# Mamba-2 mixer of a fused decoder layer: residual moved to ACT and GpSimd, and the order of the pass rewritten on five queues

## What is computed

```python
h = rmsnorm(x) * norm_w
z, xBC, dt = split(h @ in_proj_w.T)            # 1024, 1024+128+128, 16
xBC = silu(causal_conv4(xBC) + conv_b)         # depthwise, 4 taps
xs, B, C = split(xBC)
dt = softplus(dt + dt_bias); dA = exp(-exp(A_log) * dt)
state = state * dA_t + dt_t * outer(x_t, B_t)  # 16 heads of 64, state 128
y = state @ C_t + D * xs
y = rmsnorm(y * silu(z)) * ssm_norm_w
h1 = x + y @ out_proj_w.T
```

## Time and profile before

| what | us |
|---|---|
| median of 3 runs | 2724.34 (2722.08 to 2725.27) |
| the profiled execution, its own time | 2722.0 |
| span of the profiled execution | 2720.2 |
| PE busy | 2659.7 (98%) |
| DVE busy | 1523.4 (56%) |
| ACT busy | 1019.5 (37%) |
| POOL busy | 693.8 (26%) |

### The profile page before, as it was taken

One profiled execution on the slowest core, in us unless ns is written; L12 is line 12 of the kernel. 1 busy time (PEld: TensorE's weight loads), 2 busy tenths in 40 slices (PEclk: granted clock), 3 DMA queues, 4 the chain that ended last, 5 costly groups with the idle time before them and its releaser, 6 DMA issues.

```text
span 2720.2 us, 42348 instructions
## 1 busy us (share of the span) xinstructions
PE 2659.7 (98%) x15264; PEld 2070.4 (76%) x15264; DVE 1523.4 (56%) x2561; ACT 1019.5 (37%) x2375; POOL 693.8 (26%) x594
## 2 busy tenths in 40 slices
PE   7999999999999999999999989999999999999999
PEld 5777777777778888888888867777777777777776
DVE  8787797797795322332233277777777774111122
ACT  6334334334434222122212255555555553222221
POOL 6553553553561101000100101322233322000000
PEclk9999999999999999999999999999999999999999
DMA  4001001101114101110111211110111124211111
GB/s 154 27 21 47 31 15 46 44 3 46 46 48 140 62 1 62 62 62 0 62 62 48 73 70 48 63 40 29 62 54 62 58 64 150 82 47 46 46 46 47
DMA packets 85482, 147.83 MB, mean 54 GB/s; under 512 B 4032, under 2 KB 17984, under 8 KB 85408
## 3 DMA queue, kind: packets, MB, share of 16 engines
q1 hardware_dynamic: 85408, 146.84, 15.7%
HBM read 113.27 MB, written 33.55 MB: 54 GB/s over the span
## 4 chain that ended last, share of the span: by engine, by line
PE 88%; DVE 8%; issue 2%; ACT 1%; DMA 1%; DVEq 0%; SPq 0%; POOL 0%; ACTq 0%; POOLq 0%
PE ps L75 22%; PE ps L77 22%; PE ps L76 22%; PE ps L1770 4%; PE ps L2133 4%; PE ps L816 2%; PE ps L1782 2%; PE ps L1761 2%; DVE mx_m L608 1%; DVE mx_cv L600 1%; PE ps L792 1%; PE ps L804 1%; PE ps L747 1%; PE ps L1714 1%; PE ps L844 1%
## 5 line engine op out<-in xcount | busy, mean ns | idle before, releaser
L1471 ACT ACTIVATE at_pr<-ps,at_nm 128x256 f32<-128x256 f32 x512 | 235.6, 473 | 201.7 <-DVE at_nm L1621 201.7
L1162 DVE TENSOR_TENSOR gm_m_lo<-gm_m,gm_m_hi 128x512 fp32r<-128x512 f32 (+1 forms) x88 | 61.1, 694 | 416.9 <-ACT gm_m_hi L1079 416.9
L75 PE MATMUL ps<-sh_u_hi,gm_gu_hi 128*128 128x512 f32 (+1 forms) x704 | 274.9, 390 | 0.0
L76 PE MATMUL ps<-sh_u_lo,gm_gu_hi 128*128 128x512 f32 (+1 forms) x704 | 274.8, 390 | 0.0
L77 PE MATMUL ps<-sh_u_hi,gm_gu_lo 128*128 128x512 f32 (+1 forms) x704 | 274.7, 390 | 0.0
L1627 DVE COPY at_pT<-ps 128x512 f32<-128x512 f32 x256 | 176.3, 689 | 138.5 <-PE ps L1770 136.4
L1073 ACT ACTIVATE gm_sg<-ps 128x512 f32<-128x512 f32 (+1 forms) x88 | 52.7, 599 | 517.6 <-PE ps L77 517.4
L543 POOL TENSOR_TENSOR mx_m<-mx_m,mx_g 128x512 f32<-128x512 f32 x128 | 185.4, 1448 | 86.3 <-DVE mx_m L610 86.1
L75 PE MATMUL ps<-sh_u_hi,qm_w_hi 128*128 128x512 f32 x512 | 201.6, 394 | 2.1 <-issue 1.1
L77 PE MATMUL ps<-sh_u_hi,qm_w_lo 128*128 128x512 f32 x512 | 199.6, 390 | 0.0
L76 PE MATMUL ps<-sh_u_lo,qm_w_hi 128*128 128x512 f32 x512 | 199.4, 389 | 0.0
(11 more groups left out here) (252 smaller groups left out, 6352.6 us busy)
## 6 DMA issues: line engine op xcount, KB each, us to landing
sh_xf<-x_scratch SPq DMA_DIRECT2D x16, 1024.0 KB, 7.5
mx_xr<-in_x SPq DMA_DIRECT2D x8, 1024.0 KB, 5.6
h_scratch<-mx_xr SPq DMA_DIRECT2D x8, 1024.0 KB, 5.1
sh_xf<-h_scratch SPq DMA_DIRECT2D x8, 1024.0 KB, 8.4
gm_xr<-in_x SPq DMA_DIRECT2D x8, 1024.0 KB, 7.3
gm_r<-h_scratch SPq DMA_DIRECT2D x8, 1024.0 KB, 6.1
x_scratch<-gm_r SPq DMA_DIRECT2D x8, 1024.0 KB, 5.2
at_cf<-in_ctxT SPq DMA_DIRECT2D x16, 512.0 KB, 3.9
```

The costliest lines, as they stand in the source:

```text
L75: nc.tensor.matmul(out, l_hi, r_hi, start=first, stop=False)
L76: nc.tensor.matmul(out, l_hi, r_lo, start=False, stop=False)
L1471: A(pr[h][:, t, :], SC[h][:, SEQ * t:SEQ * t + SEQ], ACT.Exp, bias=nm[:, 4 * n + h, t:t + 1], accum_out=sums[:, 2 * b + t, 4 * g + h:4 * g ...
```

## The change

Residual: ACT scales the output product from PSUM into SBUF buffers `m0` (`scale_out`, two tiles behind the last work of a pass and two inside the next), POOL adds them to the input rows, in the order of tiles 2, 3, 0, 1; PE's projections n = 2 to 5 each wait for their own bank. Pass 7 keeps the old form. The squares of the next pass's input go from the convolutions into the head loop (j = 0 to 3), POOL's `first` goes behind head 9, and the normalisation goes from one tile at j = 1 to 4 to two tiles each at j = 5 and j = 6. DVE's `g_low(j - 1)` goes ahead of `scan(2j + 2)`, and PE's `chunk_out(j - 1)` ahead of `spread(2j + 4)`. The product of B and C goes ahead of projection 6, the first two spreads ahead of projection 8, the first two scans ahead of convolution 8. Convolution 9 goes on DVE behind the first gating, its SiLU on ACT behind the second.

```diff
@@ -343,9 +343,12 @@
...
-             "dac tap cv sl Ge z xd sc M t g gs glo acc sse rg h1").split()
+             "dac tap cv sl Ge z xd sc M t g gs glo acc sse rg ho h1").split()
...
+    OUT = (2, 3, 0, 1)
 
     def ahead(i):
 
@@ -462,6 +465,14 @@
             act.wait_ge(s["u"], i + 1)
             A(d["ln"], d["u"], ACT.Ln).then_inc(s["ln"], 1)
 
+        def scale_out(i, n):
+
+            t = OUT[n]
+            act.wait_ge(s["out"], KI * i + KI)
+            act.wait_ge(s["y"], KI * i + KI)
+            act.wait_ge(s["rg"], i + 1)
+            A(m0[t][:, :], ps[t][:, :], ACT.Copy, scale=rg[:, t:t + 1]).then_inc(s["ho"], 1)
+
         def main(i):
             if step_0(i):
                 take_dt(i)
@@ -469,12 +480,15 @@
             tap(i, 0)
             if step_0(i):
                 exp_ln(i)
+            else:
+                scale_out(i - 1, 2)
+                scale_out(i - 1, 3)
             tap(i, 1)
             act.wait_ge(s["dta"], i + 1)
             A(d["da"], d["dta"], ACT.Exp).then_inc(s["da"], 1)
             silu(i, 0)
             for n in range(2, NCONV - 1):
-                if n == NCONV - 2:
+                if n == NCONV - 3:
 
                     act.wait_ge(s["G"], i + 1)
                     at(act, s["M"], 2 * NH * i)
@@ -484,12 +498,9 @@
                 silu(i, n - 1)
                 if step_0(i):
                     wt.high(act, min(3 * KD + 2 * (n - 1), IN_PIECES))
-                if n >= 5:
-                    square(i + 1, n - 5)
+            zsilu(i, 0)
             silu(i, NCONV - 2)
-            zsilu(i, 0)
             tap(i, NCONV - 1)
-            silu(i, NCONV - 1)
             for j in range(KI):
                 if j + 1 < KI:
                     zsilu(i, j + 1)
@@ -504,14 +515,21 @@
                 else:
                     at(act, s["acc"], 7 * i + j - 1)
                 A(acc[:, :] if j == 0 else sq[:, :], zs[j % 2][:, :], ACT.Square).then_inc(s["gs"], 1)
-                if 1 <= j <= TT:
-                    norm(i + 1, j - 1)
+                if j == 1:
+                    silu(i, NCONV - 1)
+                if j < TT:
+                    square(i + 1, j)
+                elif j in (5, 6):
+                    norm(i + 1, 2 * j - 10)
+                    norm(i + 1, 2 * j - 9)
                 if final(i) and j >= 1:
 
                     me.nxt.wt.high(act, j if j <= 4 else 4 + 2 * max(j - 5, 0))
             if not final(i):
                 take_dt(i + 1)
                 exp_ln(i + 1)
+                scale_out(i, 0)
+                scale_out(i, 1)
 
         first(0)
         steps(act, main)
@@ -536,7 +554,6 @@
 
                 pool.wait_ge(su.small, smalls)
                 wt.by_pool(pool, len(pieces))
-            first(i + 1)
             pool.wait_ge(s["Ge"], 2 * i + 2)
             for h in range(NH):
                 pool.wait_ge(s["sc"], NH * i + h + 1)
@@ -544,10 +561,17 @@
                 G(m1[h % 4][:, :], m1[h % 4][:, :], g1[:, :], ALU.mult).then_inc(s["M"], 1)
                 if h % 2 == 1 and h >= 5:
                     add_squares(i, (h - 3) // 2)
+                if h == 9:
+                    first(i + 1)
             add_squares(i, 7)
-            at(pool, s["h1"], TT * i)
+            at(pool, s["ho"], TT * i)
             pool.wait_ge(s["sse"], i + 1)
             G(rg[:, :], v0[:, :], mhalf[:, :], ALU.pow).then_inc(s["rg"], 1)
+            if not final(i):
+                pool.wait_ge(s["xr"], 16 * i + 16)
+            for n, t in () if final(i) else enumerate(OUT):
+                pool.wait_ge(s["ho"], TT * i + n + 1)
+                G(xr[:, t, :], xr[:, t, :], m0[t][:, :], ALU.add).then_inc(s["h1"], 1)
 
         pool.wait_ge(su.dve, dve_0 + 4)
         first(0)
@@ -603,6 +627,9 @@
         def scan(i, h):
 
             dve.wait_ge(s["bc"], NH * i + h + 1)
+            if h == 0:
+
+                at(dve, s["h1"], TT * i)
             at(dve, s["y"], KI * i + h // 2 - 1)
             bank = BC[h % 2]
             V.tensor_tensor_scan(m0[h % 4][:, :], bank[:, :], eye0[:, :], 0.0, ALU.mult, ALU.add)
@@ -681,20 +708,20 @@
             for b in range(2):
                 V.memset(daT[0:2 * NH, SEQ * b:SEQ * b + 1].bitcast(F32), 0.0).then_inc(s["dac"], 1)
             for n in range(6, NCONV - 1):
+                if n == NCONV - 2:
+                    scan(i, 0)
+                    scan(i, 1)
                 conv(i, n)
                 if step_0(i):
                     wt.low(dve, 3 * KD + n - 1)
-            scan(i, 0)
-            scan(i, 1)
             scale_x(i, 0)
-            conv(i, NCONV - 1)
             if step_0(i):
                 wt.low(dve, IN_PIECES)
             for j in range(KI):
+                if j >= 1:
+                    g_low(i, j - 1)
                 if j + 1 < KI:
                     scan(i, 2 * j + 2)
-                if j >= 1:
-                    g_low(i, j - 1)
                 if j == KI - 1:
                     split(i + 1, 0)
                     split(i + 1, 1)
@@ -708,6 +735,8 @@
                 dve.wait_ge(s["z"], KI * i + j + 1)
                 dve.wait_ge(s["t"], KI * i + j + 1)
                 V.tensor_tensor(zs[j % 2][:, :], xc[:, j, :], zs[j % 2][:, :], ALU.mult).then_inc(s["g"], 1)
+                if j == 0:
+                    conv(i, NCONV - 1)
                 if final(i) and 2 <= j <= 5:
                     me.nxt.wt.low(dve, j - 1)
             split(i + 1, 2)
@@ -721,10 +750,12 @@
             V.tensor_scalar(v0[:, :], Y[:, 0:TT], 1.0 / DI, RMS_EPS, ALU.mult, ALU.add).then_inc(s["sse"], 1)
             if not final(i):
                 dt_second(i + 1)
-            dve.wait_ge(s["out"], KI * i + KI)
-            dve.wait_ge(s["xr"], 16 * i + 16)
-            dve.wait_ge(s["rg"], i + 1)
-            for t in range(TT):
+            if final(i):
+
+                dve.wait_ge(s["out"], KI * i + KI)
+                dve.wait_ge(s["xr"], 16 * i + 16)
+                dve.wait_ge(s["rg"], i + 1)
+            for t in range(TT) if final(i) else ():
                 V.scalar_tensor_tensor(xr[:, t, :], ps[t][:, :], rg[:, t:t + 1], xr[:, t, :], ALU.mult,
                                        ALU.add).then_inc(s["h1"], 1)
 
@@ -764,10 +795,10 @@
         def conv_in(i, n, also=None):
             if step_0(i) and n % 4 == 2:
                 pe.wait_ge(*wt.lows(n // 4 * KD + 2 * KD - 1))
+            if 2 <= n <= 5:
+                at(pe, s["ho"], TT * (i - 1) + n - 1)
             if n >= 4:
                 pe.wait_ge(s["cv"], 3 * NCONV * i + 3 * (n - 3))
-            elif n == 2:
-                at(pe, s["h1"], TT * i)
             project(CB[n], E_X + P * CH[n], also).then_inc(s["in"], 1)
 
         def z_in(i, c):
@@ -866,8 +897,6 @@
             for t in range(TT):
                 last = T.transpose(Y[0:2 * NH, P * t:P * t + P], da_hl[:, t, :].bitcast(F32), ident[:, :])
             last.then_inc(s["dat"], 1)
-            for n in range(6, NCONV - 2):
-                conv_in(i, n)
 
             at(pe, s["sc"], NH * i)
             pe.wait_ge(s["sl"], NCONV * i + 2)
@@ -876,10 +905,12 @@
                 T.matmul(BC[0][:, o:o + SEQ], bT[:, o:o + P], cT[:, o:o + SEQ], start=True, stop=True)
                 last = T.matmul(BC[1][:, P * b:P * b + P], bT[:, o + P:o + SEQ], cT[:, o + P:o + SEQ], start=True, stop=True)
             last.then_inc(s["G"], 1)
+            for n in range(6, NCONV - 2):
+                conv_in(i, n)
+            spread(i, 0)
+            spread(i, 1)
             conv_in(i, NCONV - 2)
             z_in(i, 0)
-            spread(i, 0)
-            spread(i, 1)
             conv_in(i, NCONV - 1)
             turn_x(i, 0)
             spread(i, 2)
@@ -896,10 +927,10 @@
                 else:
                     turn(i + 1, 2)
                     turn(i + 1, 3)
+                if j >= 1:
+                    chunk_out(i, j - 1)
                 if j + 2 < KI:
                     spread(i, 2 * j + 4)
-                if j >= 1:
-                    chunk_out(i, j - 1)
             if final(i):
                 chunk_out(i, KI - 1)
             else:
```

## The result

The changed kernel takes 2734.47 us in the median of 6 runs (2732.89 to 2738.84), the kernel before 2724.35 (2721.6 to 2725.27): a ratio of 1.0043, 95% interval 1.003 to 1.0056. The change costs 10.1 us. The profiled executions differ by 12.5 us, 2734.53 against 2722.0.

What follows compares the result with a forecast made beforehand. PE, busy 2659.7 of 2720.2 us, bounds the kernel. Pass 0 +0.7, passes 1 to 6 +6.0, pass 7 +3.8: together +10.5 us, taking the median from 2724.3 to 2734.8 us; range 2726 to 2743.

Steps and rivals of the forecast that it cites:

- The norms: Next pass's first transpose waits for ACT's two norms behind chunk 6: +1.7 us a pass, bounds +1.3 to +2.1.
- The opening: Head loop up to z_in(3): POOL's product wait goes, z_in(3) waits 0.6 us for scale_x(2); -0.7 us a pass.
- The residual: Turn of the pass: moving DVE's four instructions to ACT and POOL costs 0 and is worth nothing.
- From z_in(3) on: Chunks behind z_in(3): PE's work a chunk is the same set; cost 0, about 1 us to spare.
- Pass 7: Late tenth SiLU delays the next stage's weight load, so turn_x(3) waits: +2.8 us once (2.3 to 4.3).
- nothing behind it that could absorb it: Behind the norm wait, splits, chunk_out(7) and sums all follow from that transpose, so its +1.7 us a pass counts fully.
- Pass 0: z_in(3) starts right behind scale_x(2), -1.0 us, and the norm wait adds +1.7: together +0.7 us.
- (B): Rival: the opening opens fully, 1.9 to 2.0 us in each of 8 passes; 2724.7 us; chance 0.17 with mixtures.
- (C): Rival: POOL holds the port when g_low(0) comes, 0.85 us a pass, opening gives nothing; 2741.6 us; chance 0.14.
- (D): Rival: no norm wait, or pass 0 gains more; 2721.2 us, down to 2708 with (B); chance 0.07 of faster.
- (E): Rival: residual's move misses its purpose; if its chain held PE at conv_in(2), up to 4 us; no own chance.

Runs made afterwards that it cites:

- the kernel with three costs undone: Changed kernel with all norms behind chunk 5, pass 7's weight rounding and subtracting one chunk later, PE's spread before output product: 2721.11 us, ratio 0.9992.

## Why the prediction was right

Predicted 2734.8 us, measured 2734.47; the profiled execution 2732.5, measured 2734.53. By its steps:

- **The norms**, +1.7 a pass: 1.71 between the starts on PE, 1.80 a pass when it was taken away, 1.78 when it was put into the kernel before. Shown from three sides.
- **The opening**, -0.7: measured -0.77. `g_low(0)` started 42.40 us behind v0, forecast 269.08 - 226.66 = 42.42; `turn_x(2)` 43.90, as forecast. Waits of 0.74 at `turn_x(2)` (0.7) and 0.35 at `z_in(3)` (0.6).
- **The residual**, 0: shown to be 0 in the loop.
- **From z_in(3) on**, 0: wrong by 0.22 us a pass, 1.3 us in six. I had noted that PE's work a chunk is the same set, and costed its new order at nothing. Putting the spread back took this stretch to 31.92 us, against 31.89 before.
- **Pass 7**, +2.8 for the load: measured 1.7 as a wait, 1.8 between the starts of z_in(3) and z_in(4) (9.91 against 8.12 in the loop). The mechanism was right (ACT stood 2.04 us for the DMA, and without it both waits go), the landing was mis-sized: I took 3.2 us, and it was 2.6 from the SiLU's end (790.06 + 0.62 = 790.68) to ACT's start at 793.32, just below the 2.7 at the low end of the earlier trace rows. That is 0.7 of the 1.0 missing; the rest is small differences of both arrivals. A second term failed here: "nothing behind it that could absorb it". In pass 7 of the kernel before PE waits 0.4 us for DVE's split at the second group of these transposes (L747, at 823.26), and in the changed kernel that wait is gone. From the first transpose to v0 pass 7 took 10.53 us before and takes 10.12, so of the norm wait 0.4 was absorbed.
- **Pass 0**, +0.7: measured +0.5. z_in(3) started at 71.66 with a wait of 0.40 for `scale_x(2)`, 1.42 sooner than 73.08 where 1.0 was forecast; the norms cost 1.7 and the stretch from z_in(3) 0.2, as in the loop.
- **Later stages**, not in the sum: +1.9. The granted clock in two stretches of the attention's start, for the changed kernel, shows where 1.6 of it may lie:

```profile
1593.60:1597.00 3.40, 3.40 (x10) 2.66 (x9) 1.33 (x3) 0.00 (x0) 0.00 (x0) 0.53 1.00 286
...
1610.70:1614.10 3.40, 3.40 (x14) 2.72 (x12) 0.69 (x1) 2.27 (x10) 0.00 (x0) 0.52 0.00 0
```

The kernel before has one such stretch there, at 1594.5, and none later in that stage. The change doesn't bring the second: the kernel with convolution 9 back ahead of the loop has a single one, at 1608.5, and took 1889.4 us behind its last v0; the kernel before with late norms has one too and took 1889.0. So the 1.9 belongs to the execution and not to the change.

So of the agreement of the totals a part is luck: the mixer was forecast at +10.5 and gave +10.6, the passes of the loop more than forecast (7.5 against 6.0) and pass 7 less (2.6 against 3.8). The medians differ by 10.1 and the profiled executions by 12.5, so 0.3 us between forecast and median is closer than either can tell.

Of the rivals, (B) fell with the opening's two waits; (C) with its rows: `g_low(0)` took 0.68 us at 270.84, with POOL idle from 269.3; (D) with the norm wait; (E) inside the loop, where the residual back on DVE left the distance of the passes as it was.

## What to carry over

Ahead of every move of work on a side engine ask at which instruction of the bounding engine its result is due, and from which event of that engine it is itself released: the two norms hung on the gating of the last chunk but one and were due 0.8 us after it was released. On a kernel whose PE is 98% busy, put a small job between two such points into the chunk before, where the side engine stands idle for 3 us. When a wait is moved on one of two engines that hand work to each other, as rounding and subtracting a weight piece, move the other with it.

## What was not expected of the hardware

A wait of PE can cost more than it shows. Behind waits of 1.9 to 2.8 us PE was at times granted about half of its clock (0.50 to 0.56 in the windows shown) for a stretch of about 3.4 us, which made a pass 1.6 to 1.7 us longer; behind the same 2.8 us in other passes of the same execution it kept 1.00. No pass of the loop with waits of at most 1.6 us, in the profiles of eleven such kernels, showed it. But such a wait is no safeguard outside the loop: in pass 0 of the kernel with three costs undone the longest wait in the 20 us ahead of the stretch at 70.5 is 1.3 us. What decides between two like passes stays open.

DVE's low half and GpSimd's product (L543, now L560) stretched each other where they met: the product has a mean of 1448 ns before and 1285 in the changed kernel, the low half 1133 and 689. With the low half ahead of the scans it falls into the stretch in which GpSimd is idle. That is 28 us of DVE and 21 of GpSimd saved by order: with the old order of low half and output product and all else as changed, the means are 1133 and 1422 again. The shorter instructions as such show nothing in the time, since neither engine bounds the kernel; what the order gives there is the earlier start of `g_low(0)`.
